# Layernorm statistics: the sum of squares moves from ScalarE to VectorE, and the negated mean times rstd moves the other way

## The chip, the cores and the metric

The kernel runs on the 8 cores of one Trainium2 chip. Each core takes one batch element of the input (4096 tokens of 1024 features) and runs the same program. No core waits for another. The time is the device time of the slowest core in microseconds (us), and smaller is better.

## What is computed

One layer of two sub-layers, each with a layernorm in front and a layernorm behind, and a residual. The layernorm has no gain and no bias:

```python
def _layernorm(x, axis=-1, eps=1e-5):
    m = jnp.mean(x, axis=axis, keepdims=True)
    v = jnp.var(x, axis=axis, keepdims=True)
    return (x - m) / jnp.sqrt(v + eps)
...
x = x + _layernorm(_L0_attn_ref(_layernorm(x), W_q, W_k, W_v, W_o))
x = x + _layernorm(_L0_ffn_ref(_layernorm(x), gate_w, We1, ..., Ws2, bs2))
```

`_L0_attn_ref` is causal linear attention with one head of 64: q and k go through elu + 1, a running sum of the outer products of k and v is read out with q and divided by a running normalizer. `_L0_ffn_ref` is a mixture of 16 experts (2 per token, chosen by a softmax gate) and one shared expert, each a gated MLP in a hyperbolic geometry.

## The kernel before

All work is tiled by 128 tokens, one token per partition, so 32 tiles per core. Every instruction is written out once by hand through a helper, `kb.op(engine, emit, after, inc)`: it appends to the list of one engine ("T" TensorE, "V" VectorE, "S" ScalarE, "G" GpSimd, "Y" SyncE, which issues most DMAs), and an engine runs its list strictly in order. `after` holds what the instruction waits for, also where that lies on its own engine. The profile calls the engines PE, DVE, ACT, POOL and SP.

There are four stages, one after another:

- **Stage A1** (`a1_tile` and `a2_chunk`, interleaved by tile). `a1_tile(i)` loads 128 x 1024 of x (L449), takes its statistics with `ln_stats`, normalizes on ScalarE (L456), transposes on TensorE (L462), and makes q, k and v. `phi` (L409 to L418) is elu + 1: VectorE, an Exp on ScalarE (L412), VectorE. `a2_chunk(i-1)` follows with the attention of the tile before it. There are two x buffers and one of nearly everything else.
- **Stage A3** (L603 to L790). For each tile: the output projection into PSUM (L625, L630), a copy to SBUF `s_at` (L642), `ln_stats` over it, x plus bias on ScalarE (L693), the residual on VectorE (L697, a scalar_tensor_tensor of two fp32 SBUF tensors, into `s_x`), `ln_stats` over that result, its normalization on ScalarE (L711), eight fp32 transposes (L721), two copies out of PSUM (L727, L730), and the gate (L747 and the small VectorE operations up to L788).
- **FFN**, in two halves of 16 tiles. It doesn't call `ln_stats`.
- **Final**, after each FFN half, 16 tiles: load x (L1176), `ln_stats` over the FFN output `s_y`, x plus bias on ScalarE (L1181), the residual on VectorE (L1185), the store (L1188). Load and store are issued from the same SyncE list, and the load of a tile stands behind the store of the tile before.

`ln_stats(src_ap, cb, variant, after_src)` writes a few 128x1 columns `C(cb)` to `C(cb+7)` of one small tile `s_c`, and returns rstd and minus mean times rstd. It is called 32 times in A1, 64 times in A3 (variant "expln": Ln, then Exp with factor -0.5, L391 and L394) and 32 times in the final stage (variant "sqrt": Sqrt and reciprocal, L398 and L401). Its two wide operations are the sum (L375, VectorE) and the sum of squares (L378, ScalarE, whose elementwise output goes to the scratch tile `s_sqs`). The small ones are L381 (mean), L384 (its square), L387 (variance) and L403 (minus mean times rstd), all on VectorE.

Beside A1 and the first half of A3, GpSimd converts the fp32 expert weights to bf16: it loads a chunk, casts it from SBUF to SBUF (L284, 128x3328) and stores it, 72 times. The FFN waits for all of it, and for the end of A3.

Of the kernel before, what the change touches and what calls it, by code (L numbers as in the profile page):

```python
# [10 lines left out]
AF = mybir.ActivationFunctionType  # L11
ALU = mybir.AluOpType
AX = mybir.AxisListType

B, T, D, H = 8, 4096, 1024, 64
# [176 lines left out]
def build_nc(debug=False, stop_after=None, a3_gate=True, a3_xtspill=True,  # L192
# [4 lines left out]
    kb = KB(nc, es)  # L197
# [38 lines left out]
    chV = kb.chan("chV", "V")  # L236
    chS = kb.chan("chS", "S")
# [7 lines left out]
    s_sqs = es.enter_context(st("s_sqs", [128, D], BF16))  # L245
# [17 lines left out]
    def C(i):  # L263
        return s_c[:, i:i + 1]
# [59 lines left out]
    for dsrc, dst in ((d_wq, s_wqb), (d_wk, s_wkb), (d_wv, s_wvb)):  # L324
        tin = kb.op("Y", lambda y, s=dsrc: y.dma_start(out=s_wst[:, 0:512], in_=s),
                    after=(prev[0],), inc=chL[0], k=16)
        tcv = kb.op("G", lambda gp, d=dst: gp.tensor_copy(out=d[:, :], in_=s_wst[:, 0:512]),
                    after=(tin,), inc=chGc)
# [3 lines left out]
                after=(prev[0],), inc=chL[0], k=16)  # L332
    tcv = kb.op("G", lambda gp: gp.tensor_copy(out=s_wob[:, :], in_=s_wst[:64, 0:1024]),
                after=(tin,), inc=chGc)
# [4 lines left out]
    if stop_after == "W":  # L339
        kb.op("G", lambda g: g.nop(),  # L340
              after=(prev[0], prev[1], t_consts[0]))
# [32 lines left out]
    def ln_stats(src_ap, cb, variant, after_src):  # L374
        t1 = kb.op("V", lambda v: v.tensor_reduce(  # L375
            out=C(cb), in_=src_ap, axis=AX.X, op=ALU.add),
            after=after_src, inc=chV)
        t2 = kb.op("S", lambda s: s.activation(  # L378
            out=s_sqs[:, :], in_=src_ap, func=AF.Square, accum_out=C(cb + 1)),
            after=after_src, inc=chS)  # L380
        t3 = kb.op("V", lambda v: v.tensor_scalar(  # L381
            out=C(cb + 2), in0=C(cb), scalar1=1.0 / D, scalar2=None,
            op0=ALU.mult), after=(t1,), inc=chV)
        t4 = kb.op("V", lambda v: v.tensor_tensor(  # L384
            out=C(cb + 3), in0=C(cb + 2), in1=C(cb + 2), op=ALU.mult),
            after=(t3,), inc=chV)
        t5 = kb.op("V", lambda v: v.scalar_tensor_tensor(  # L387
            out=C(cb + 4), in0=C(cb + 1), scalar=1.0 / D, in1=C(cb + 3),
            op0=ALU.mult, op1=ALU.subtract), after=(t2, t4), inc=chV)
        if variant == "expln":  # L390
            t6 = kb.op("S", lambda s: s.activation(  # L391
                out=C(cb + 5), in_=C(cb + 4), func=AF.Ln, bias=c_epsln),
                after=(t5, t_cst), inc=chS)
            t7 = kb.op("S", lambda s: s.activation(  # L394
                out=C(cb + 6), in_=C(cb + 5), func=AF.Exp, scale=c_mhalf),
                after=(t6,), inc=chS)
        else:
            t6 = kb.op("S", lambda s: s.activation(  # L398
                out=C(cb + 5), in_=C(cb + 4), func=AF.Sqrt, bias=c_epsln),
                after=(t5, t_cst), inc=chS)  # L400
            t7 = kb.op("V", lambda v: v.reciprocal(  # L401
                out=C(cb + 6), in_=C(cb + 5)), after=(t6,), inc=chV)
        t8 = kb.op("V", lambda v: v.tensor_scalar(  # L403
            out=C(cb + 7), in0=C(cb + 2), scalar1=C(cb + 6), scalar2=-1.0,
            op0=ALU.mult, op1=ALU.mult), after=(t7, t4), inc=chV)
        return C(cb + 6), C(cb + 7), (t7, t8)

    def phi(src_ap, dst_ap, w, after, np_=128):
# [212 lines left out]
    for i in range(NT):  # L621
        p = i % 2
        cb = 32 * p
# [4 lines left out]
            after=(tok_o[i], g_at[p]) + ((g_of, g_oc) if i < 2 else ()),  # L628
            inc=None)
        t2 = kb.op("T", lambda t, i=i, atp=atp: t.matmul(  # L630
            atp[:, 512:1024], s_of[0:64, i * 128:(i + 1) * 128],
            s_wob[:, 512:1024], start=True, stop=True), after=(), inc=chT)
        if a3_level < 2:
            tev = kb.op("V", lambda v, atp=atp, p=p: v.tensor_copy(
                out=s_w32[:, p * D:(p + 1) * D], in_=atp[:, :]),
                after=(t2, g_at[p], g_w32[p]), inc=chV)
# [6 lines left out]
            out=atsl, in_=atp[:, :]), after=(t2, g_at[p], g_atS[p]), inc=chV)  # L643
        g_at[p] = tat
        if 11 <= a3_level <= 15:
            toks = []
            t1 = kb.op("V", lambda v, atsl=atsl, cb=cb: v.tensor_reduce(
                out=C(cb), in_=atsl, axis=AX.X, op=ALU.add),
                after=(tat,), inc=chV)
            toks.append(t1)  # L650
            if a3_level >= 12:
                t2s = kb.op("S", lambda s, atsl=atsl, cb=cb: s.activation(
                    out=s_sqs[:, :], in_=atsl, func=AF.Square,
                    accum_out=C(cb + 1)), after=(tat,), inc=chS)
                toks.append(t2s)
            if a3_level >= 13:
                t3 = kb.op("V", lambda v, cb=cb: v.tensor_scalar(
                    out=C(cb + 2), in0=C(cb), scalar1=1.0 / D, scalar2=None,
                    op0=ALU.mult), after=(t1,), inc=chV)
                t4 = kb.op("V", lambda v, cb=cb: v.tensor_tensor(  # L660
                    out=C(cb + 3), in0=C(cb + 2), in1=C(cb + 2), op=ALU.mult),
                    after=(t3,), inc=chV)
                t5 = kb.op("V", lambda v, cb=cb: v.scalar_tensor_tensor(
                    out=C(cb + 4), in0=C(cb + 1), scalar=1.0 / D,
                    in1=C(cb + 3), op0=ALU.mult, op1=ALU.subtract),
                    after=(t2s, t4), inc=chV)
                t8 = kb.op("V", lambda v, cb=cb: v.tensor_scalar(
                    out=C(cb + 7), in0=C(cb + 2), scalar1=C(cb + 4),
                    scalar2=-1.0, op0=ALU.mult, op1=ALU.mult),
                    after=(t5,), inc=chV)  # L670
                toks += [t8]
            if a3_level >= 14:
                t6 = kb.op("S", lambda s, cb=cb: s.activation(
                    out=C(cb + 5), in_=C(cb + 4), func=AF.Ln, bias=c_epsln),
                    after=(t5, t_cst), inc=chS)
                t7 = kb.op("S", lambda s, cb=cb: s.activation(
                    out=C(cb + 6), in_=C(cb + 5), func=AF.Exp, scale=c_mhalf),
                    after=(t6,), inc=chS)
                toks += [t7]
            tev = kb.op("V", lambda v, atsl=atsl, p=p: v.tensor_copy(  # L680
                out=s_w32[:, p * D:(p + 1) * D], in_=atsl),
                after=tuple(toks) + (g_w32[p],), inc=chV)
# [7 lines left out]
            out=xsl, in_=d_x[i * 128:(i + 1) * 128, :]),  # L690
            after=(g_x[p],), inc=chX[p], k=16)
        wsl = s_w32[:, p * D:(p + 1) * D]
        txf = kb.op("S", lambda s, xsl=xsl, wsl=wsl, mb=mb: s.activation(  # L693
            out=wsl, in_=xsl, func=AF.Identity, bias=mb),
            after=(tx, tln[1], g_w32[p]), inc=chS)
        tx2 = kb.op("V", lambda v, atsl=atsl, xsl=xsl, wsl=wsl, rstd=rstd:
                    v.scalar_tensor_tensor(  # L697
                        out=xsl, in0=atsl, scalar=rstd, in1=wsl,
                        op0=ALU.mult, op1=ALU.add),
                    after=(txf, tln[0]), inc=chV)  # L700
        g_atS[p] = tx2
        tok_x2sp[i] = kb.op("Y", lambda y, i=i, xsl=xsl: y.dma_start(
            out=d_x2[i * 128:(i + 1) * 128, :], in_=xsl),
            after=(tx2,), inc=chSp[p], k=16)
        if a3_level < 3:
# [6 lines left out]
                                   scale=rstd2, bias=mb2),  # L712
                      after=tln2 + (txf,), inc=chS)
# [6 lines left out]
        for k in range(8):  # L720
# [3 lines left out]
                after=(tln2f, g_tr2) if k == 0 else (),  # L724
                inc=chT if k == 7 else None)
        g_w32[p] = ttr
        tfm32 = kb.op("V", lambda v: v.tensor_copy(  # L727
            out=s_fm32[:, :], in_=p_tr2[:, :]), after=(ttr, g_fm32), inc=chV)
        bsl = s_b16[:, p * D:(p + 1) * D]
        txtb = kb.op("V", lambda v, bsl=bsl: v.tensor_copy(  # L730
            out=bsl, in_=p_tr2[:, :]),
            after=(ttr, g_b16[p], tfm32), inc=chV)
        g_tr2 = txtb
        if a3_xtspill:
            tok_xtsp[i] = kb.op("Y", lambda y, i=i, bsl=bsl: y.dma_start(
                out=d_xt[:, :, i * 128:(i + 1) * 128].rearrange("k p n -> p k n"),
                in_=bsl.rearrange("p (k n) -> p k n", k=8)),
                after=(txtb,), inc=chXt[p], k=16)
# [7 lines left out]
        for k in range(8):  # L746
# [3 lines left out]
                after=(tfm32, g_gate) if k == 0 else (),  # L750
                inc=chT if k == 7 else None)
# [3 lines left out]
            out=gsl, in_=p_gate[:, :]), after=(tg, g_gate), inc=chV)  # L755
        tmx = kb.op("V", lambda v, cb=cb, gsl=gsl: v.reduce_max(
            out=C(cb + 16), in_=gsl, axis=AX.X), after=(tgc,), inc=chV)
        tnm = kb.op("V", lambda v, cb=cb: v.tensor_scalar(
            out=C(cb + 17), in0=C(cb + 16), scalar1=-1.0, scalar2=None,
            op0=ALU.mult), after=(tmx,), inc=chV)  # L760
# [3 lines left out]
            out=esl, in_=gsl, func=AF.Exp, bias=C(cb + 17)),  # L764
            after=(tnm,), inc=chS)
        g_gate = tgc
        tse = kb.op("V", lambda v, cb=cb, esl=esl: v.tensor_reduce(
            out=C(cb + 18), in_=esl, axis=AX.X, op=ALU.add),
            after=(te,), inc=chV)
        trs = kb.op("V", lambda v, cb=cb: v.reciprocal(  # L770
            out=C(cb + 19), in_=C(cb + 18)), after=(tse,), inc=chV)
        tm1 = kb.op("V", lambda v, cb=cb, esl=esl: v.reduce_max(
            out=C(cb + 20), in_=esl, axis=AX.X), after=(te,), inc=chV)
        teq = kb.op("V", lambda v, cb=cb, esl=esl, bsl2=bsl2: v.tensor_scalar(
            out=bsl2, in0=esl, scalar1=C(cb + 20), scalar2=None,
            op0=ALU.is_equal), after=(tm1,), inc=chV)
        tmk = kb.op("V", lambda v, esl=esl, bsl2=bsl2: v.scalar_tensor_tensor(
            out=bsl2, in0=bsl2, scalar=-1e30, in1=esl,
            op0=ALU.mult, op1=ALU.add), after=(teq,), inc=chV)
        tm2 = kb.op("V", lambda v, cb=cb, bsl2=bsl2: v.reduce_max(  # L780
            out=C(cb + 21), in_=bsl2, axis=AX.X), after=(tmk,), inc=chV)
        th = kb.op("V", lambda v, cb=cb, esl=esl, i=i: v.tensor_scalar(
            out=s_hit[:, i * 16:(i + 1) * 16], in0=esl, scalar1=C(cb + 21),
            scalar2=None, op0=ALU.is_ge), after=(tm2,), inc=chV)
        tw1 = kb.op("V", lambda v, cb=cb, esl=esl, bsl2=bsl2: v.tensor_scalar(
            out=bsl2, in0=esl, scalar1=C(cb + 19), scalar2=None,
            op0=ALU.mult), after=(trs, tm2), inc=chV)
        tw2 = kb.op("V", lambda v, i=i, bsl2=bsl2: v.tensor_tensor(  # L788
            out=s_wte[:, i * 16:(i + 1) * 16], in0=bsl2,
            in1=s_hit[:, i * 16:(i + 1) * 16], op=ALU.mult),  # L790
            after=(th, tw1), inc=chV)
# [6 lines left out]
    if stop_after == "A":  # L798
        kb.op("G", lambda g: g.nop(), after=a_done)
        with nc.Block() as block:  # L800
# [21 lines left out]
                   after=a_done, inc=chGc)  # L822
    t_ones_time = kb.op("G", lambda g: g.memset(s_timeb[:, :], 1.0),
                        after=a_done, inc=chGc)
# [285 lines left out]
    for h in range(2):  # L1110
        yg = tuple(t for t in g_y if t is not None)
        ty0 = kb.op("G", lambda g: g.memset(s_y[:, :], 0.0),
                    after=yg + ((a_done) if h == 0 else ()), inc=chGc)
        ty1 = kb.op("G", lambda g: g.memset(
            bass.AP(s_y, 0, [[NLT * D, 128], [D, NLT], [1, 1]]), 1.0),
            after=(ty0,), inc=chGc)
# [52 lines left out]
        for lt in range(NLT):  # L1169
            gi = h * NLT + lt  # L1170
            px = lt % 2
            cb = 32 * px + 16
# [4 lines left out]
                out=xsl, in_=d_x2[gi * 128:(gi + 1) * 128, :]),  # L1177
# [55 lines left out]
```

How the kernel before makes its waits and increments, by code:

```python
            def section(eng, items=items, engname=engname):  # L91
                waited = {}
                for _, after, emitfn, inc, k, idx in items:
                    for (ch, tidx) in after:
                        if ch.owner == engname == "T":
                            continue
                        val = val_at[(ch.name, tidx)]
                        if waited.get(ch.name, 0) < val:
                            eng.wait_ge(ch.sem, val)
                            waited[ch.name] = val
                    instr = emitfn(eng)
                    if inc is not None:
                        if instr is None:
                            instr = eng.nop()
                        instr.then_inc(inc.sem, k)
```

## Time and profile before

| | us |
|---|---|
| device time, median of 2 runs | 7313.36 (7301.6 to 7325.12) |
| device time of the profiled execution | 7106.19 |
| its span, slowest core | 7104.5 |
| spans of the 8 cores | 7075.2 to 7104.5 |
| mean granted TensorE clock of the cores | 0.761 to 0.775 |
| busy: PE, DVE, ACT, POOL | 4617.9, 3785.3, 3425.4, 322.4 |

The profile is of one execution, 207 us shorter than the median of the timed runs. Its busy shares (PE 65%, DVE 53%, ACT 48%) are means over stages that have nothing in common: A1 takes about 22 to 632 us, A3 632 to 1383 us, the two FFN halves about 1400 to 4118 and 4260 to 6982 us, and the two final stages 4118 to 4243 and 6982 to 7104.5 us. So what an edit is worth is read stage by stage. "Waits" of an engine are put down to the instruction whose semaphore came last.

### The profile page before, as it was taken

The numbers are of one execution on the slowest core, as the hardware profiler recorded it, in microseconds if no ns is written. First come the engines' busy times: TensorE is split into PE (matmuls) and PEld (weight loads), VectorE is DVE, ScalarE is ACT, GpSimd is POOL, SyncE is SP. The second block draws the span as 40 slices with busy tenths as digits, with TensorE's granted clock in tenths as the row PEclk, the third lists the DMA queues.
The fourth block names the chain that finished last, engine by engine and source line by source line (L and its number), as shares of the span: only waits on it lengthen the run. The fifth ranks groups of instructions, "written<-read, shape, count | busy, mean of one in ns | idle before, by whom it ended". The sixth has DMA issues, their size and how long they took to land.

```text
span 7104.5 us, 86704 instructions; the slowest of 8 cores (7075.2 to 7104.5 us)
## 1 busy us (share of the span) xinstructions
PE 4617.9 (65%) x27904; PEld 2811.3 (40%) x27904; DVE 3785.3 (53%) x8768; ACT 3425.4 (48%) x6077; POOL 322.4 (5%) x238
## 2 busy tenths in 40 slices
PE   2232222387777887777886718877778887778672
PEld 2222222254444454444553405544445544445350
DVE  3444554455555555555554345555555555555434
ACT  1112222255555555565554335556655555565434
POOL 2222210000000000000000000000000000000000
PEclk8555555588888888887887858888878888888786
DMA  5666741211111111111111031111111111121102
GB/s 208 221 222 222 239 157 59 96 53 50 44 44 66 51 54 47 44 44 66 53 33 52 13 124 64 53 47 44 44 67 55 53 44 44 44 69 33 55 16 92
DMA packets 371414, 547.20 MB, mean 77 GB/s; under 512 B 48338, under 2 KB 327250, under 8 KB 357394
## 3 DMA queue, kind: packets, MB, share of 16 engines
q1 hardware_dynamic: 350226, 358.49, 15.7%
q0 software_dynamic: 20736, 183.18, 7.2%
q8 instruction: 224, 3.67, 0.2%
q14 instruction: 228, 1.87, 0.1%
HBM read 438.62 MB, written 103.00 MB: 76 GB/s over the span
## 4 chain that ended last, share of the span: by engine, by line
ACT 34%; PE 32%; DVE 19%; issue 10%; DMA 3%; DVEq 1%; ACTq 1%; SPq 1%; POOL 0%; POOLq 0%
ACT s_sqs L1029 9%; ACT s_sqs L1054 9%; ACT s_y L1087 8%; PE psA L896 5%; PE psB L896 5%; PE psB L907 5%; PE psA L907 5%; PE p_s1C L896 2%; DMA s_x<-x2sp 2%; DVE s_c L1077 2%; DVE s_c L375 2%; ACT s_c L1068 2%; PE p_s3C L907 2%; PE p_gate L747 2%; ACT s_sq L945 1%
## 5 line engine op out<-in xcount | busy, mean ns | idle before, releaser
L1001 PE MATMUL psB<-s_we,s_sf 128*128 128x512 bf16 (+1 forms) x2048 | 679.0, 490 | 310.5 <-DVE s_w L1042 310.5
L1001 PE MATMUL psA<-s_we,s_sf 128*128 128x512 bf16 (+1 forms) x2048 | 687.6, 496 | 286.3 <-DVE s_w L1042 265.0
L1087 ACT ACTIVATE s_y<-s_w,s_c 128x1024 f32<-128x1024 f32 x544 | 624.6, 1148 | 356.2 <-DVE s_c L1077 353.1
L924 ACT ACTIVATE s_a<-s_s1f,s_beb 128x256 bf16<-128x256 f32 x1152 | 490.8, 496 | 532.9 <-DVE s_s1f L918 531.7
L896 PE MATMUL psA<-s_xtb,s_we 128*128 128x256 bf16 x4096 | 544.3, 299 | 228.7 <-DMA s_xtb<-xtsp 171.9
L945 ACT ACTIVATE s_sq<-s_sf 128x1024 bf16<-128x1024 bf16 (+1 forms) x272 | 301.0, 1107 | 761.6 <-DVE s_sf L940 744.5
L907 PE MATMUL psA<-s_xtb,s_we 128*128 128x256 bf16 x4096 | 536.0, 296 | 168.4 <-DVE s_w L1042 168.4
L1029 ACT ACTIVATE s_sqs<-s_b 128x1023 bf16<-128x1023 bf16 x544 | 575.3, 1058 | 96.3 <-DVE s_b L1026 95.2
L896 PEld LDWEIGHTS psA<-s_xtb,s_we 128*128 128x128 bf16 x4096 | 428.5, 107 | 353.8 <-issue 272.8
L1054 ACT ACTIVATE s_sqs<-s_w 128x1023 bf16<-128x1023 f32 x544 | 566.8, 1042 | 0.5
L907 PEld LDWEIGHTS psA<-s_xtb,s_we 128*128 128x128 bf16 x4096 | 432.9, 106 | 255.5 <-issue 176.0
L1001 PEld LDWEIGHTS psB<-s_we,s_sf 128*128 128x128 bf16 x2048 | 218.3, 116 | 748.7 <-issue 645.9
L1001 PEld LDWEIGHTS psA<-s_we,s_sf 128*128 128x128 bf16 x2048 | 220.5, 117 | 723.7 <-issue 625.8
L896 PE MATMUL psB<-s_xtb,s_we 128*128 128x256 bf16 x4096 | 469.1, 273 | 1.9 <-DMA s_xtb<-xtsp 1.9
L907 PE MATMUL psB<-s_xtb,s_we 128*128 128x256 bf16 x4096 | 468.1, 273 | 0.0
L896 PEld LDWEIGHTS psB<-s_xtb,s_we 128*128 128x128 bf16 x4096 | 393.1, 98 | 67.8 <-issue 23.9
L907 PEld LDWEIGHTS psB<-s_xtb,s_we 128*128 128x128 bf16 x4096 | 401.1, 98 | 46.1
L1026 DVE CAST s_b<-psA 128x1023 bf16<-128x1023 f32 x256 | 312.3, 1220 | 145.0 <-PE psA L1011 143.6
L721 PE MATMUL p_tr<-s_idf,s_w 128*128 128x128 f32 x256 | 62.1, 424 | 495.2 <-ACT s_w L711 495.2
L1068 ACT ACTIVATE s_c<-s_c 128x1 f32<-128x1 f32 x544 | 110.3, 203 | 490.3 <-DVE s_c L1066 490.3
L933 DVE TENSOR_SCALAR s_s3b<-psB,s_beb 128x256 bf16<-128x256 f32 x512 | 212.2, 477 | 229.8 <-PE psB L907 224.4
L933 DVE TENSOR_SCALAR s_s3b<-psA,s_beb 128x256 bf16<-128x256 f32 x512 | 212.2, 477 | 228.8 <-PE psA L907 228.8
(171 smaller groups left out, 6523.7 us busy)
## 6 DMA issues: line engine op xcount, KB each, us to landing
s_xtb<-xtsp SPq DMA_DIRECT2D x272, 512.0 KB, 3.8
s_we<-wec SPq DMA_DIRECT2D x32, 3326.8 KB, 11.5
s_wst<-wexp POOLq DMA_DIRECT2D x48, 1664.0 KB, 8.9
wec<-s_wsb POOLq DMA_DIRECT2D x48, 832.0 KB, 4.5
s_x<-x SPq DMA_DIRECT2D x64, 512.0 KB, 5.0
s_wst<-wexp POOLq DMA_DIRECT2D x16, 1661.5 KB, 9.3
x2sp<-s_x SPq DMA_DIRECT2D x32, 512.0 KB, 2.6
s_x<-x2sp SPq DMA_DIRECT2D x32, 512.0 KB, 4.3
```

Of the source, the lines that this page charges most:

```text
L375: t1 = kb.op("V", lambda v: v.tensor_reduce(out=C(cb), in_=src_ap, axis=AX.X, op=ALU.add), after=after_src, inc=chV)
L896: t.matmul(s1r[:, it * GRP:(it + 1) * GRP], wsl[:, w1o + k * stride1 + it * 128: w1o + k * stride1 + it * 128 + 128], xsl[:, k * GRP:(k + ...
L907: t.matmul(s3r[:, it * GRP:(it + 1) * GRP], wsl[:, w3o + k * stride1 + it * 128: w3o + k * stride1 + it * 128 + 128], xsl[:, k * GRP:(k + ...
L924: s.activation(out=s_a[:, it * GRP:(it + 1) * GRP], in_=s_s1f[:, (it - it0) * GRP:(it - it0 + 1) * GRP], func=AF.Silu, bias=bsl[:, it:it + ...
L933: v.tensor_scalar(out=s_s3b[:, it * GRP:(it + 1) * GRP], in0=s3r[:, it * GRP:(it + 1) * GRP], scalar1=bsl[:, nit + it:nit + it + 1], scala ...
L945: tsq = kb.op("S", lambda s, sfo=sfo, nit=nit, pg=pg: s.activation(out=s_sq[:, pg * 2048:pg * 2048 + nit * GRP], in_=s_sf[:, sfo:sfo + nit ...
L1001: wnh=wnh, pob=pob: t.matmul(pob(nh * 512, nh * 512 + wnh), s_sf[:, sfo + kt * GRP + tt * 128: sfo + kt * GRP + tt * 128 + 128], wsl[:, w2 ...
L1026: v.tensor_copy(out=bscr, in_=pob(0, NSH)),
L1029: s.activation(out=s_sqs[:, 0:NSH], in_=bscr, func=AF.Square, accum_out=C(cb)),
L1054: tS1 = kb.op("S", lambda s, zsl=zsl, cb=cb: s.activation(out=s_sqs[:, 0:NSH], in_=zsl[:, 1:D], func=AF.Square, accum_out=C(cb + 2)), afte ...
L1068: tsq2 = kb.op("S", lambda s, cb=cb: s.activation(out=C(cb + 7), in_=C(cb + 6), func=AF.Sqrt), after=(trc,), inc=chS)
L1087: s.activation(out=ysl, in_=zsl, func=AF.Identity, scale=rcol),
```

## The change

Only `ln_stats` changes. The sum of squares becomes a VectorE scalar_tensor_tensor, (x * 1.0) * x, with an accumulator output. The mean column becomes the negated mean. In the variant "expln" the product of negated mean and rstd is now a ScalarE Identity with a per-partition scale; in the variant "sqrt" it stays on VectorE. The square of the mean and the variance are computed as before.

```diff
-        t2 = kb.op("S", lambda s: s.activation(
-            out=s_sqs[:, :], in_=src_ap, func=AF.Square, accum_out=C(cb + 1)),
-            after=after_src, inc=chS)
+        t2 = kb.op("V", lambda v: v.scalar_tensor_tensor(
+            out=s_sqs[:, :], in0=src_ap, scalar=1.0, in1=src_ap,
+            op0=ALU.mult, op1=ALU.mult, accum_out=C(cb + 1)),
+            after=after_src, inc=chV)
         t3 = kb.op("V", lambda v: v.tensor_scalar(
-            out=C(cb + 2), in0=C(cb), scalar1=1.0 / D, scalar2=None,
+            out=C(cb + 2), in0=C(cb), scalar1=-1.0 / D, scalar2=None,
             op0=ALU.mult), after=(t1,), inc=chV)
...
             t7 = kb.op("S", lambda s: s.activation(
                 out=C(cb + 6), in_=C(cb + 5), func=AF.Exp, scale=c_mhalf),
                 after=(t6,), inc=chS)
+            t8 = kb.op("S", lambda s: s.activation(
+                out=C(cb + 7), in_=C(cb + 2), func=AF.Identity,
+                scale=C(cb + 6)), after=(t7,), inc=chS)
         else:
...
             t7 = kb.op("V", lambda v: v.reciprocal(
                 out=C(cb + 6), in_=C(cb + 5)), after=(t6,), inc=chV)
-        t8 = kb.op("V", lambda v: v.tensor_scalar(
-            out=C(cb + 7), in0=C(cb + 2), scalar1=C(cb + 6), scalar2=-1.0,
-            op0=ALU.mult, op1=ALU.mult), after=(t7, t4), inc=chV)
+            t8 = kb.op("V", lambda v: v.tensor_scalar(
+                out=C(cb + 7), in0=C(cb + 2), scalar1=C(cb + 6), scalar2=None,
+                op0=ALU.mult), after=(t7,), inc=chV)
```

## Rows read from the trace of the kernel before

**Rows 1.** Busy time by stretch: stretch, its length, then each engine's busy us (instructions).

```profile
22.00:632.00 610.00, 187.02 (x1794) 147.00 (x1794) 275.03 (x897) 119.52 (x257) 185.03 (x138) 0.61 0.62 222
...
1000.00:1372.00 372.00, 103.80 (x417) 82.93 (x416) 179.58 (x438) 104.03 (x187) 0.00 (x0) 0.50 0.19 59
```

**Rows 2.** Chain of waits, one tile of A3: start us, us, what.

```profile
1143.44 1.30 DVE s_x L697
...
1144.83 1.23 DVE s_c L375
...
1161.24 1.23 DVE s_c L375
...
1164.13 0.23 DVE s_c L403
...
1165.75 1.29 DVE s_x L697
```

**Rows 3.** Timeline of the same ln_stats in A3: start us, us, engine line operation.

```profile
1161.23 1.06 ACT L378 ACTIVATE s_sqs<-s_at 128x1024 bf16<-128x1024 f32 x1 [3.51 <-DVE s_at L642]
...
1162.19 0.19 ACT L378 ACTIVATION_READ_ACCUMULATOR s_sqs<-s_at 128x1 f32 x1
1162.56 0.15 DVE L381 TENSOR_SCALAR s_c<-s_c 128x1 f32<-128x1 f32 x1
...
1163.34 0.29 ACT L391 ACTIVATE s_c<-s_c,s_cst 128x1 f32<-128x1 f32 x1 [0.96 <-DVE s_c L387]
1163.73 0.29 ACT L394 ACTIVATE s_c<-s_c,s_cst 128x1 f32<-128x1 f32 x1
...
1164.49 1.15 ACT L693 ACTIVATE s_w<-s_x,s_c 128x1024 f32<-128x1024 f32 x1 [0.47 <-DVE s_c L403]
```

**Rows 4.** Timeline of an ln_stats in A1, and the square of the next tile.

```profile
419.33 1.20 DVE L375 TENSOR_REDUCE s_c<-s_x 128x1 f32<-128x1024 f32 x1
420.64 0.15 DVE L381 TENSOR_SCALAR s_c<-s_c 128x1 f32<-128x1 f32 x1
...
432.10 1.04 ACT L378 ACTIVATE s_sqs<-s_x 128x1024 bf16<-128x1024 f32 x1
```

**Rows 5.** Durations by line: ns min/median/max, first and last start us.

```profile
L697 DVE SCALAR_TENSOR_TENSOR s_x<-s_at,s_c,s_w x32: 1283/1285/2472, 637.4 to 1367.0; 128x1024 f32<-128x1024 f32 x32
...
L387 DVE SCALAR_TENSOR_TENSOR s_c<-s_c 128x1 f32<-128x1 f32 x34 | 5.4, 160 | 3.9 <-DVE s_c L384 0.5
...
L378 ACT ACT_TABLE_LOAD  x1: 1283/1283/1283, 22.9 to 22.9; - x1
```

**Rows 6.** Timeline, two wide VectorE operations with no wait between them (FFN).

```profile
4099.00 1.23 DVE L1026 CAST s_b<-p_s1C 128x1023 bf16<-128x1023 f32 x1
4100.14 1.21 DVE L1042 SCALAR_TENSOR_TENSOR s_w<-p_s1C,s_y 128x1023 f32<-128x1023 f32 x1
```

**Rows 7.** A cast of GpSimd beside VectorE in A1 (timeline), and all casts by line.

```profile
398.31 2.96 POOL L284 CAST s_wsb<-s_wst 128x3328 bf16<-128x3328 f32 x1 [7.88 <-DMA s_wst<-wexp]
...
398.79 2.48 DVE L384 TENSOR_TENSOR s_c<-s_c 128x1 f32<-128x1 f32 x1
...
L284 POOL CAST s_wsb<-s_wst x72: 2102/2960/3225, 30.2 to 987.3; 128x3328 bf16<-128x3328 f32 x55, 128x3323 bf16<-128x3323 f32 x16, 128x2295 bf16<-128x2295 f32 x1
```

**Rows 8.** Groups by line, 22:632, then 632:1000: count, busy us, mean ns.

```profile
L384 DVE TENSOR_TENSOR s_c<-s_c 128x1 f32<-128x1 f32 x32 | 27.6, 864 | 3.3
...
L384 DVE TENSOR_TENSOR s_c<-s_c 128x1 f32<-128x1 f32 x30 | 22.9, 762 | 3.3 <-DVE s_c L381 0.3
```

**Rows 9.** Timeline of a tile of the final stage; the last row is another tile.

```profile
4210.72 1.21 DVE L375 TENSOR_REDUCE s_c<-s_y 128x1 f32<-128x1024 f32 x1
...
4213.48 0.21 DVE L403 TENSOR_SCALAR s_c<-s_c 128x1 f32<-128x1 f32 x1
4215.89 1.15 ACT L1181 ACTIVATE s_w<-s_x,s_c 128x1024 f32<-128x1024 f32 x1 [2.78 <-DMA s_x<-x2sp]
...
7088.83 1.15 ACT L1181 ACTIVATE s_w<-s_x,s_c 128x1024 f32<-128x1024 f32 x1 [2.24 <-DMA s_x<-x2sp]
```

## The prediction, made before the changed kernel was run

> **What bounds the kernel now.** The change touches only `ln_stats`, so I first cut the span at the calls of it, with the busy time by stretch [rows 1]. In A1 (22 to 632 us) PE is busy 187 of 610 us, DVE 275 and ACT 120. In the later part of A3 it is alike: 104, 180 and 104 of 372 us. No engine is near its limit, so these stages are bound by a chain in which one engine at a time works. The two long FFN stretches hold no `ln_stats`; I expect nothing there.
>
> Second, the chain of waits for one tile of A3 [rows 2]. From one residual operation L697 to the next it is 1143.44 to 1165.75, 22.31 us, a tile of A3. Both calls of `ln_stats` lie on the chain: the sum L375 at 1144.83 and at 1161.24, and L403 at 1164.13. The square L378 is nowhere on it.
>
> Third, the timeline, to see why the square is off it [rows 3]. In A3 it starts at 1161.23, together with the sum. Its accumulator is read by 1162.38, before the sum ends (1161.24 + 1.23 = 1162.47). In A1 the square of a tile even runs before its sum: at 432.10, while DVE is busy with the tile before [rows 4]. So in both stages the square is work on ACT that costs nothing today.
>
> **The new square on DVE.** It has the same start condition as the sum and stands right behind it, so now it stands in line with it. The price of the instruction: L697 is a scalar_tensor_tensor over two fp32 SBUF inputs of 1024 columns and takes 1285 ns [rows 5]; it reads its scalar from SBUF. The new one has an immediate scalar. L403 has its scalar in SBUF and takes 0.21 us [rows 9] where L381 with an immediate takes 0.15 [rows 3], so some 60 ns come off: 1.225 us, which is also what the wide sum takes. Two wide DVE operations with no wait between them overlap: L1042 starts 1.14 us behind the start of L1026, which lasts 1.23 [rows 6].
>
> Then the start of the next instruction, L381. Today it is 1.32 us behind the start of the sum (1161.24 to 1162.56 [rows 2, 3]; in A1 419.33 to 420.64 [rows 4]), since it waits for the sum's result. After the change the sum takes 1.14 us to the start of the square, and the square 1.14 us to L381, which waits for nothing any more: 2.28. That is 0.96 us more. To it comes the read of the accumulator. No row shows one on DVE. The nearest is ACT's: it starts 0.10 us before the square ends and lasts 0.19 [rows 3], so it adds 0.09. From below it is 0. From above it is a small DVE operation with a full wait in front, 0.16 + 0.10 and a little more, say 0.35. I take 0.09, by the nearest row: **1.05 us per call** (0.96 to 1.31). L384 and L387 follow as before; the squares' sum is there by the time L387 needs it (two small operations later).
>
> On the path: 32 calls in A1 and 64 in A3, 96 x 1.05 = 100.8 us (92 to 126).
>
> **The product on ACT.** Today from the start of L394 to the start of L693 it is 1163.73 to 1164.49, 0.76 us, with a hop to DVE and back [rows 3]. After the change L394 is followed by another small ACT operation and then by the wide one. The step from one small ACT operation to the next that waits for it is 0.39 us (L391 to L394 [rows 3]). Twice that is 0.78, so +0.02 per call, 96 x 0.02 = 2 us: the hop saved and the operation added cancel. The new Identity reads an SBUF operand besides its input, as L391 and L394 do, so I keep their price. It could be a tenth of a microsecond cheaper (as a DVE operation with an immediate is 0.06 cheaper than one without) or 0.02 dearer: -7 to +4.
>
> **The table load.** ACT's first table load now stands before L391 of the first tile instead of beside the first sum [rows 5], 1.28 us, of which some was already on the path: +1, once.
>
> **GpSimd's casts.** A small DVE operation with two SBUF inputs that becomes due during a cast waits for its end: L384 at 398.79 lasts 2.48 us and ends at 401.27, the very end of the cast that began at 398.31 [rows 7]. The new square has two SBUF inputs. There are 72 casts in 957 us [rows 7], 0.075 per us. L384 loses (864 - 160) x 32 = 22.5 us in A1 and (762 - 160) x 30 = 18.1 us in A3 up to 1000 us [rows 8]. Three parts: a cast that hit L384 now hits the square, due some 0.45 us earlier, about 9 casts, +4 us. A cast that comes due during the square waits for it and then holds L384 for up to 2.7 us: 62 squares (32 in A1, 30 in A3 [rows 8]) x 1.23 us x 0.075 = 5.7 casts at 2.5 = +14 us. And the longer tiles take up casts that would have cost about 1 us each elsewhere (62 x 1.05 x 0.075 = 5): -5. Sum **+13 us** (0, if the casts fall between, to 25). GpSimd itself is no path: its last cast starts at 987 us [rows 7], and L697 still runs at 1367 [rows 5].
>
> **The final stage.** The load of x ends the wait there: L1181 starts at 4215.89 on the DMA, and L403 has been ready since 4213.69 [rows 9]. That leaves 2.2 us of cover for 1.05 more. In a tile with a faster load ACT sat idle 2.24 us instead of 2.78, so 1.66 us of cover. Without this cover it would cost 32 x 1.05 = 34 us. I take 0.
>
> **What ACT gains**: 128 squares of 1.04 to 1.06 us and their reads, 128 x (1.05 + 0.19) = 159 us of busy time off ACT. But all of it ran while ACT would have waited anyway [rows 2 to 4]. Worth 0.
>
> **Sum**: 100.8 + 2 + 1 + 13 = 117 us. Against the profiled execution: 7106.2 + 117 = 7223. The timed runs' median is 207 us above it; I can't tell from the trace where those lie, and both A stages are chains of fixed latencies, so I add the same 117 to the median: 7313.4 + 117 = **7430 us**, +1.6%. From the bounds: 92 - 7 + 0 + 0 = 85 to 126 + 4 + 1 + 25 = 156 us, and 12 us either way for the scatter of the two runs around their median: 7386 to 7481.
>
> **Rivals.**
>
> *The accumulating form runs at half the rate.* For: no row shows a DVE operation with an accumulator, and it has to keep two fp32 streams and a running sum. Against: L697 has the same two streams and shows one column per cycle. Its price: the width-dependent part of the square is 1.225 - 0.160 (L387, one column [rows 5]) = 1.065 us, so it comes on top once more: 2.12 us per call, 96 x 2.12 = 203 us. Casts hit a square twice as long: 25 us. The final stage's cover of 1.66 to 2.2 us is used up in part, about 3 us. With 2 and 1 it is 234 us: 7547 us, +3.2%, slower. It decides from 1.35 us per call on ((146 - 16) / 96, where 146 us are 2%).
> The Trainium skill says this in so many words (Vector Engine (DVE) Microarchitecture Reference, section Points that are easy to get wrong): a scalar_tensor_tensor with two non-bf16 SBUF sources runs at half throughput, since both read ports are taken and none is left for the accumulator. The trace does not bear out the first half of it: L697 with two fp32 SBUF sources takes 1285 ns for 1024 columns, not some 2.3 us. Whether an accumulator output brings it about no run here shows; that is what keeps this rival at more than a few per cent.
>
> *The square is hidden.* If it cost nothing, 7313. For: DVE is busy under half of these stages. Against: the sum right before it and L403 behind it are both on the chain [rows 2]. In A1 it could only hide if DVE ran it before the sum while waiting for PE, but it stands behind the sum, which stands behind the last tile's work.
>
> *The tables.* If Ln and Exp landed in different table sets now that no Square comes first, there would be two loads of 1.28 us in each of 96 calls, 246 us more: 7676. Against: today Ln and Exp run 96 times with a single load in all of A1 and A3 [rows 5].
>
> **How the numbers follow.** Forecast (0.96 to 1.31 us per call) 0.80; half rate 0.12; hidden, or something freed on ACT that I don't see, 0.04; tables 0.02; casts much worse than I reckon 0.02. The range of the forecast holds 8 in 10, so it is the range, 7386 to 7481. A measurement of this kernel tells about 2% (146 us) from no change. Slower by more than that: the half rate, the tables, the casts and the upper end of the forecast (0.11), together 0.27. Faster by over 2%: 0.01. Within 2%: 0.72.
>
> **What would show it.** In the profile of the changed kernel: a wide DVE operation at L378's place of about 1.22 us with a short accumulator read; from the start of the sum to the start of the negated mean about 2.4 us where it was 1.32; a tile of A3 without casts 24.4 to 24.5 us long instead of 22.3; the first FFN matmul some 117 us later; ACT busy some 130 us less (159 less 96 small operations of 0.29); the two FFN stretches and the final stages as long as before. I am wrong if the square takes over 1.5 us, if a table load stands between Ln and Exp, or if the FFN stretches change.

## The result, and the profile after

| | before | after |
|---|---|---|
| ratio of the times, 95% interval | | 1.0129 (1.0083 to 1.0175) |
| device time of the profiled execution, us | 7106.19 | 7218.57 |
| span, mean of the 8 cores, us | 7088.4 | 7193.4 |
| median of all timed runs, us | 7167.91 (10 runs) | 7344.12 (11 runs) |
| busy PE, DVE, ACT, us | 4617.9, 3785.3, 3425.4 | 4612.0, 3896.2, 3313.4 |

The change makes the kernel 1.3% slower, some 92 us of 7106. In part of the executions, of either kernel, the cores of one die or of both show a lower granted TensorE clock (0.72 against 0.76 in the one of 7344.12 us) and the time is 1 to 5% longer, so the ratio leaves those executions out, and by their times the two behind the 7313 us that stood ahead of the prediction are among them.

To see where the time goes I use one mark that every core has: the first clearing of `s_y` by GpSimd, which waits for the end of A3. Here is its row in before, by line (count, ns min/median/max, start of the first and of the last, of the slowest core):

```profile
L1112 POOL MEMSET s_y<- x2: 13745/13748/13751, 1385.6 to 4243.9; 128x16384 f32 x2
```

The same row in after, also of the slowest core:

```profile
L1116 POOL MEMSET s_y<- x2: 13745/13748/13751, 1479.0 to 4342.8; 128x16384 f32 x2
```

| mean of the 8 cores, us | before | after | difference |
|---|---|---|---|
| A3 begins (first L642, now L646) | 627.0 | 664.6 | +37.6 |
| A3 ends (first clearing of `s_y`) | 1380.8 | 1473.2 | +92.4 |
| second half begins (second clearing) | 4230.5 | 4329.6 | +99.1 |
| end of the span | 7088.4 | 7193.4 | +105.0 |

So 92 us arise in A1 and A3. The other 13 us lie in the two FFN halves, where the program is the same. In before the rest of the program behind A3 took 5708 us and in after 5720. In the profiled executions of the experiments below that leave this part alone it took 5698 to 5721 us (5698 in prod_act_only, 5707 in sq_dve_only, 5721 in sums_act_dmacast1), and 5769 and 5761 in before_dmacast and before_dmacast1, where after_dmacast, with the same edit, took 5719. That is no relation to the edits, so I put these 13 us down to the scatter between executions. The final stages stayed as they were: from their first to their last wide ScalarE operation 113.3 us before and 112.8 after in the first half, 111.1 and 112.3 in the second (means of the cores).

The timeline of after shows the same stretch of a tile of A3 as [rows 2] and [rows 3] (lines behind L378 are shifted: L381 is now L382, L387 L388, L391 L392, L394 L395, L693 L697, L697 L701; L398 is the new product):

```profile
1234.24 1.22 DVE L375 TENSOR_REDUCE s_c<-s_at 128x1 f32<-128x1024 f32 x1
1235.37 1.22 DVE L378 SCALAR_TENSOR_TENSOR s_sqs<-s_at 128x1024 bf16<-128x1024 f32 x1
1236.51 0.08 DVE L378 DVE_READ_ACCUMULATOR s_sqs<-s_at 128x1 f32 x1
1236.51 0.15 DVE L382 TENSOR_SCALAR s_c<-s_c 128x1 f32<-128x1 f32 x1
...
1237.03 0.16 DVE L388 SCALAR_TENSOR_TENSOR s_c<-s_c 128x1 f32<-128x1 f32 x1
1237.29 0.29 ACT L392 ACTIVATE s_c<-s_c,s_cst 128x1 f32<-128x1 f32 x1 [6.57 <-DVE s_c L388]
1237.67 0.29 ACT L395 ACTIVATE s_c<-s_c,s_cst 128x1 f32<-128x1 f32 x1
1238.06 0.29 ACT L398 ACTIVATE s_c<-s_c 128x1 f32<-128x1 f32 x1
1238.50 1.15 ACT L697 ACTIVATE s_w<-s_x,s_c 128x1024 f32<-128x1024 f32 x1
1239.76 1.29 DVE L701 SCALAR_TENSOR_TENSOR s_x<-s_at,s_c,s_w 128x1024 f32<-128x1024 f32 x1 [2.57 <-ACT s_w L697]
```

From the start of the sum to the start of the mean it is now 2.27 us (1234.24 to 1236.51); it was 1.32 [rows 3]. The square is in line, 0.95 us per call. The read of the accumulator is an instruction of its own of 0.08 us, but it has the same start as L382: it costs nothing. From the Exp to the wide operation it is 0.83 us (1237.67 to 1238.50) where it was 0.76 [rows 3].

By line, the square of after and its accumulator read (ns min/median/max):

```profile
L378 DVE SCALAR_TENSOR_TENSOR s_sqs<-s_x x64: 1202/1215/3683, 25.0 to 1462.0; 128x1024 bf16<-128x1024 f32 x64
L378 DVE DVE_READ_ACCUMULATOR s_sqs<-s_x x64: 70/77/84, 26.1 to 1463.1; 128x1 f32 x64
```

The median is 1215 ns for 1024 columns. The maximum of 3683 is a square that waited for a cast, as the small operation L384 did in [rows 7].

### The profile page after: what moved, and what is told of

The parts are those of the page before. It is cut to its first block, busy times and chain, and to the rows that moved or that the text cites. A ratio compares the mean times of both kernels' runs of the same rounds, so it can differ in the third digit from the quotient of the medians.

```text
span 7217.0 us, 86276 instructions; the slowest of 8 cores (7178.0 to 7217.0 us)
## 1 busy us (share of the span) xinstructions
PE 4612.0 (64%) x27764; PEld 2822.4 (39%) x27904; DVE 3896.2 (54%) x8928; ACT 3313.4 (46%) x5917; POOL 326.9 (5%) x238
## 4 chain that ended last, share of the span: by engine, by line
ACT 34%; PE 32%; DVE 18%; issue 12%; DMA 3%; DVEq 1%; ACTq 1%; SPq 0%; POOL 0%; POOLq 0%
ACT s_sqs L1033 9%; ACT s_sqs L1058 9%; ACT s_y L1091 8%; PE psA L900 5%; PE psB L900 5%; PE psB L911 5%; PE psA L911 5%; PE p_s1C L900 2%; DMA s_x<-x2sp 2%; DVE s_c L375 2%; DVE s_c L1081 2%; PE p_gate L751 2%; ACT s_c L1072 2%; PE p_s3C L911 2%; ACT s_sq L949 1%
## 5 line engine op out<-in xcount | busy, mean ns | idle before, releaser
L1005 PE MATMUL psB<-s_we,s_sf 128*128 128x511 bf16 (+1 forms) x1984 | 675.4, 500 | 331.6 <-DVE s_w L1046 326.5
L1005 PE MATMUL psA<-s_we,s_sf 128*128 128x511 bf16 (+1 forms) x1984 | 663.5, 493 | 292.1 <-DVE s_w L1046 258.4
L1030 DVE CAST s_b<-psA 128x1023 bf16<-128x1023 f32 x256 | 312.3, 1220 | 150.0 <-PE psA L1015 148.6
```

The lines of the kernel that those rows point to most:

```text
L1005: wnh=wnh, pob=pob: t.matmul(pob(nh * 512, nh * 512 + wnh), s_sf[:, sfo + kt * GRP + tt * 128: sfo + kt * GRP + tt * 128 + 128], wsl[:, w2 ...
L1030: v.tensor_copy(out=bscr, in_=pob(0, NSH)),
```

## Experiments

Each kernel below differs from the kernel before, or from the changed one, by the edit shown. The mark is again the end of A3, the mean of the 8 cores of the profiled execution. In the kernels in which GpSimd casts, the 8 cores end A3 up to 25 us apart, so such a mean is known to 2 or 3 us (its standard error); where the DMAs cast one at a time in before_dmacast1 and after_dmacast1 they lie within 4.4 us, and the mean is known to 0.6.

| kernel | A3 begins | A3 ends | span |
|---|---|---|---|
| before | 627.0 | 1380.8 | 7088.4 |
| after | 664.6 | 1473.2 | 7193.4 |
| sq_dve_only | 664.2 | 1470.6 | 7177.6 |
| prod_act_only | 633.6 | 1387.6 | 7085.8 |
| before_dmacast | 575.0 | 1335.9 | 7105.1 |
| after_dmacast | 608.4 | 1403.1 | 7121.8 |
| before_dmacast1 | 575.1 | 1295.0 | 7056.1 |
| after_dmacast1 | 608.8 | 1392.1 | 7107.3 |
| final_3sq | 665.9 | 1474.6 | 7248.8 |
| a1_sum_act | 575.4 | 1335.9 | 7042.6 |
| sums_act | 576.8 | 1233.5 | 6941.2 |
| sums_act_dmacast | 537.4 | 1227.6 | 6948.7 |
| sums_act_dmacast1 | 537.0 | 1161.2 | 6882.5 |

### The two halves of the change, each alone

sq_dve_only takes only the first edit of the diff (the square on VectorE). prod_act_only takes only the negated mean and the product on ScalarE.

> Kernel before with the one edit that the sum of squares is the VectorE scalar_tensor_tensor with an accumulator output; mean and product as before. Measure: start of GpSimd's first clearing of s_y (it waits for the end of A3), mean of the 8 cores: 1380.8 us in the kernel before, 1473.2 in the changed one (+92.3). Theory (the square stands in line on VectorE, 0.95 us per call, 96 calls, and GpSimd's casts add nothing net): +85 to +91, so 1466 to 1472, and the start of the sum to the start of the mean 2.27 us. Rival (the hop to ScalarE for the product makes a good part of the loss): below +75.

> Kernel before with the one edit that the mean is negated and the product with rstd runs on ScalarE in the variant expln; the square stays on ScalarE. Theory: the step from the Exp to the wide ScalarE operation grows by 0.06 to 0.07 us, 96 calls, +6 us at the end of A3 (1387). Rival (the hop is cheaper by some 0.1 us, as the saved semaphore would suggest): -5 to -10 us.

Measured: the square alone moves the end of A3 by +89.8 us, the product alone by +6.8 us, both together by +92.4, each give or take some 3 us. The next section takes the scatter of the casts out of these three numbers. The time of sq_dve_only is 1.0143 (1.0098 to 1.0187) of before. The square is the loss; the product is a small second one. The hop that is saved is replaced by an operation that costs as much and a little more. The rivals of both expectations fall.

### The casts taken away

The question here is what GpSimd's casts add to the change. In before_dmacast and after_dmacast the weights are cast by the DMAs, so nothing reads SBUF on GpSimd beside VectorE:

```diff
-        tin = kb.op("G", lambda gp, s=src_ap, pp=p, w=width:
-                    gp.dma_start(out=s_wst[:, pp * CH:pp * CH + w], in_=s), ...)
-        tcv = kb.op("G", lambda gp, pp=p, w=width: gp.tensor_copy(...), ...)
-        tst = kb.op("G", lambda gp, d=dst_ap, pp=p, w=width:
-                    gp.dma_start(out=d, in_=s_wsb[:, pp * CH:pp * CH + w]), ...)
+        tst = kb.op("G", lambda gp, s=src_ap, d=dst_ap:
+                    gp.dma_start(out=d, in_=s),
+                    after=(tok_prev[p],), inc=chCv[p], k=16)
```

> Kernel before, but GpSimd no longer casts the weights from SBUF to SBUF: the 72 chunks are cast by the DMAs on the way from DRAM to DRAM, issued from GpSimd. Same result. Theory (a cast holds each VectorE operation with two SBUF inputs, and all of that lies on the chain of A1 and A3): the small operations like L384 drop to 0.16 us everywhere, and A3 ends some 90 us earlier, near 1290 us. Rival (the stalls lie in waits that would be there anyway): A3 ends within 10 us of 1381. If the casting DMAs are slow and end after A3, the FFN starts late and the time is longer, whatever the stalls.

> The changed kernel with the same edit to the weights as before_dmacast. Theory A (the new square costs the same with and without casts; casts add nothing net): A3 ends 96 x (0.95 + 0.065) = 97 us behind that of before_dmacast. Theory B, my prediction's (+13 us from casts that hit the square): the difference without casts is 13 us smaller than with them, 92 - 13 = 79 us.

Measured: A3 of before_dmacast begins 52.0 us earlier, but ends only 44.9 us earlier, so in A3 it lost 7 us instead of winning some 35. The waits of ScalarE in it say why (who waited for what, us in total, times, longest; the slowest core):

```profile
ACT s_w L686 <- DMA s_x<-x: 45.9, 1, 45.9
```

One load of x at the start of A3, issued at 591.92 us, held ScalarE up for 46 us (38 to 46 on the eight cores), to about the time when the last casting DMAs ended (they are issued up to 636 us). In after_dmacast that wait was 10 to 14 us. So the difference of the two in A3 (33.9 us) says nothing on the casts. A1 has no such wait, and there the difference is +33.4 us without casts and +37.6 with them. The pair doesn't decide between the theories, and its expectation missed this wait.

So the pair was repeated with one casting DMA in flight instead of two:

```diff
-                    after=(tok_prev[p],), inc=chCv[p], k=16)
+                    after=(tok_prev[p], tok_prev[1 - p]), inc=chCv[p], k=16)
```

> before_dmacast with only one casting DMA in flight at a time instead of two (each waits for the one before). Theory (the long wait of one load of x at the start of A3 comes from two casting DMAs crowding the DMA queues, and the stalls behind GpSimd's casts are 86 us): the wait goes, A3 ends 80 to 86 us before 1380.8, near 1297. Rival (any casting DMA holds a load of x until all have ended): the wait grows, since they last longer, and A3 ends behind 1336.

> after_dmacast with one casting DMA in flight. Theory A (each call costs 0.95 + 0.065 us without casts, and the casts took 9 us less in the changed kernel than in the one before): A3 ends 97 to 98 us behind that of before_dmacast1. Theory B (my prediction's +13 us for casts): 79 us.

Measured: the long wait is gone (3.2 us at most on any of the eight cores), and before_dmacast1 ends A3 at 1295.0, 85.9 us before the kernel before. The small operation that [rows 8] shows at a mean of 864 and 762 ns has no stall left in it:

```profile
L377 DVE TENSOR_TENSOR s_c<-s_c x128: 159/160/161, 27.5 to 7106.5; 128x1 f32<-128x1 f32 x128
```

after_dmacast1 ends A3 97.2 us behind before_dmacast1: theory A's 97 to 98, not theory B's 79.

A count from the traces says the same core by core. The mean of each group of VectorE operations in A1 and in A3 is compared with the mean of the same group where nothing casts on GpSimd; what is above it are stalls. Taken off the end of A3 of each core, they leave:

| mean of the 8 cores, us | stalls in A1 | stalls in A3 | end of A3 | end of A3 less the stalls |
|---|---|---|---|---|
| before | 51.8 | 34.0 | 1380.8 | 1295.0 |
| prod_act_only | 56.2 | 29.5 | 1387.6 | 1301.9 |
| sq_dve_only | 57.6 | 27.0 | 1470.6 | 1386.0 |
| after | 55.7 | 25.1 | 1473.2 | 1392.3 |
| final_3sq (the changed kernel up to here) | 57.2 | 25.9 | 1474.6 | 1391.5 |

The last number of before is that of before_dmacast1 (1295.0), and that of after is within 0.2 us of after_dmacast1 (1392.1). On the cores of before it lies between 1293 and 1298, where the ends themselves lie between 1372 and 1388. So all of the stalls lay on the chain. And the change adds up: the square alone costs 91.0 us, which is 96 x 0.95, the product alone 6.9, both 97.3.

With casts the difference at the end of A3 is 92.4 us, so the casts gave back 5 us where I had added 13. By the count it is the same: 80.9 us of stalls instead of 85.8. The minus sign is not firm: the other two executions with the square on VectorE have 83.1 and 84.6 us. The +13 is ruled out by all three.

How can that be, when the mechanism that I priced is there? This is one tile of A3 of the changed kernel, where a cast becomes due during a square:

```profile
889.45 1.22 DVE L375 TENSOR_REDUCE s_c<-s_x 128x1 f32<-128x1024 f32 x1
890.59 1.22 DVE L378 SCALAR_TENSOR_TENSOR s_sqs<-s_x 128x1024 bf16<-128x1024 f32 x1
890.64 3.98 POOL L284 CAST s_wsb<-s_wst 128x3323 bf16<-128x3323 f32 x1 [9.64 <-DMA s_wst<-wexp]
...
891.98 2.65 DVE L385 TENSOR_TENSOR s_c<-s_c 128x1 f32<-128x1 f32 x1
```

The cast takes 3.98 us instead of 2.96, since it waits for the square, and then it holds L385 for 2.65 us instead of 0.16: 2.5 us, just as I had priced it. But such a hit is no addition. By the same count L384 lost 30.8 us in before (the 40.6 that I had read in [rows 8] are of one core, this is the mean of eight); in after L385 loses 8.9 us and the square 26.8, together 4.9 more where I had reckoned 18 (+4 and +14). The other operations lost 55.0 us in before and 45.2 in after, 9.8 less where I had reckoned 5. Read together, these sums say that a cast that hits the square is for the most part one that would have hit another operation. Part of the rest is that the casts run at their own pace and end near 1000 us in either kernel, so the A3 that begins 38 us later sees about 25 of them instead of 27 ((996 - 665) / 13.3 and (987 - 627) / 13.3). How the casts fall from tile to tile was not taken apart further.

### The cover of the final stage

Here the square runs three times in a row, in the variant "sqrt" alone:

```diff
+        if variant != "expln":
+            for _r in range(2):
+                t2 = kb.op("V", lambda v: v.scalar_tensor_tensor(
+                    out=s_sqs[:, :], in0=src_ap, scalar=1.0, in1=src_ap,
+                    op0=ALU.mult, op1=ALU.mult, accum_out=C(cb + 1)),
+                    after=after_src + (t2,), inc=chV)
```

> The changed kernel, but in the final stage (variant sqrt) the square runs three times in a row on VectorE, each behind the one before. Same result. Theory (one square hides in the wait for the load of x, of which 1.66 to 2.2 us is cover): three squares delay the product by 0.95 + 2 x 1.32 = 3.6 us instead of 0.95, so about 1.4 to 1.9 us of each tile show, 21 to 29 us more per final stage (112 us from its first to its last wide ScalarE operation before and after the change). Rival (the final stage is bound by the DMAs' rate, whatever VectorE does): 112 us again.

Measured: from its first to its last wide ScalarE operation a final stage takes 137.6 us in the first half and 137.4 in the second (means of the cores), against 112.8 and 112.3 in the changed kernel: +24.8 and +25.1 us. Both are in the range. The timeline of a tile shows what ends the wait:

```profile
4245.35 0.29 ACT L408 ACTIVATE s_c<-s_c,s_cst 128x1 f32<-128x1 f32 x1 [7.04 <-DVE s_c L394]
...
4246.32 1.15 ACT L1191 ACTIVATE s_w<-s_x,s_c 128x1024 f32<-128x1024 f32 x1 [0.68 <-DVE s_c L413]
```

In [rows 9] L1181 waited for the DMA. Now the same operation waits for the product on VectorE. One square in this stage is free because of 1.7 to 2.2 us of cover, and three are not. The cover itself can be read on one core (core 0, before and after: the wide operation, and what its engine waited for, us in total and times):

```profile
L1181 ACT ACTIVATE s_w<-s_x,s_c x32: 1147/1147/1149, 4122.2 to 7096.1; 128x1024 f32<-128x1024 f32 x32
  DMA s_x<-x2sp: 82.9, 30
...
L1185 ACT ACTIVATE s_w<-s_x,s_c x32: 1147/1147/1148, 4212.5 to 7183.8; 128x1024 f32<-128x1024 f32 x32
  DMA s_x<-x2sp: 49.9, 30
```

The wait for the load is still there after the change, and 33 us shorter: 1.1 us in each of the 30 tiles.

### The opposite direction

If wide work on VectorE is on the chain and wide work on ScalarE is not, the statistics should go to ScalarE. In a1_sum_act the sum of A1 is an Identity on ScalarE with an accumulator output:

```diff
-        t1 = kb.op("V", lambda v: v.tensor_reduce(
-            out=C(cb), in_=src_ap, axis=AX.X, op=ALU.add), ...)
+        t1 = kb.op("S", lambda s: s.activation(
+            out=s_w32[:, 0:D], in_=src_ap, func=AF.Identity,
+            accum_out=C(cb)), after=after_src, inc=chS)
```

> The opposite direction, from the kernel before: in A1 the sum goes to ScalarE too (an Identity with accumulator output into a scratch tile, ahead of the square), A3 and the final stage as before. Theory (wide ScalarE work in A1 runs ahead of its tile and is free, wide VectorE work is on the chain at its full length): a tile of A1 is 1.2 to 1.3 us shorter, A3 starts 39 to 42 us earlier than 627.0, near 586. Rival (ScalarE's second pass gets in the way of the Exp of phi): A3 starts less than 20 us earlier.

Measured: A3 begins 51.6 us earlier, more than the 39 to 42 expected. The same count of stalls finds 37.6 us in its A1 instead of 51.8, so some 14 us of the gain are stalls behind casts, and 37 us, 1.2 per tile, are the sum itself. Without casts it is 38.1 us (575.1 in before_dmacast1, 537.0 in sums_act_dmacast1, whose A1 has the same edit). ScalarE does both passes in the time in which it would have waited:

```profile
307.75 1.04 ACT L376 ACTIVATE s_w<-s_x 128x1024 f32<-128x1024 f32 x1
...
308.79 1.04 ACT L385 ACTIVATE s_sqs<-s_x 128x1024 bf16<-128x1024 f32 x1
...
314.67 0.14 DVE L388 TENSOR_SCALAR s_c<-s_c 128x1 f32<-128x1 f32 x1
```

sums_act adds the same thought for A3. The copy out of PSUM moves to ScalarE and gives its sum, and the residual operation gives the sum of its result:

```diff
-        tat = kb.op("V", lambda v, atp=atp, atsl=atsl: v.tensor_copy(
-            out=atsl, in_=atp[:, :]), after=(t2, g_at[p], g_atS[p]), inc=chV)
+        tat = kb.op("S", lambda s, atp=atp, atsl=atsl, cb=cb: s.activation(
+            out=atsl, in_=atp[:, :], func=AF.Identity, accum_out=C(cb)),
+            after=(t2, g_at[p], g_atS[p]), inc=chS)
...
                         out=xsl, in0=atsl, scalar=rstd, in1=wsl,
-                        op0=ALU.mult, op1=ALU.add),
+                        op0=ALU.mult, op1=ALU.add, accum_out=C(cb + 8)),
```

> From the kernel before: A1 as in a1_sum_act; in A3 the copy of the projection out of PSUM moves to ScalarE with an accumulator output that gives its sum, the residual operation on VectorE gives the sum of its own result through its accumulator output, and both separate sums go. Same result. Theory (what counts is the length of the chain): 40 us in A1; in A3 about 2.2 us per tile for the first call (the copy no longer stands behind the gate's small operations) and 0.5 for the second, 86 us; A3 ends near 1255 us, the time is 1.7% shorter. Rival (ScalarE becomes the chain: copy and square one after the other cost what the sum saved): A3 ends above 1320.

Measured: A3 ends at 1233.5, 147 us earlier, 21 more than expected. Without casts the same edits make it 133.8 us (1295.0 in before_dmacast1, 1161.2 in sums_act_dmacast1), so some 14 us of the 21 came with the casts; the other 8 were not looked into. The device time of the profiled execution is 6950.68 against 7109.88 in one of the kernel before on the same chip, 2.2% less; for this pair there is no interval. The timeline of a tile of A3:

```profile
1156.00 1.00 ACT L649 ACTIVATE s_at<-p_at 128x1024 f32<-128x1024 f32 x1
...
1157.18 1.06 ACT L385 ACTIVATE s_sqs<-s_at 128x1024 bf16<-128x1024 f32 x1
...
1158.17 0.18 DVE L796 TENSOR_TENSOR s_wte<-s_g16b,s_hit 128x16 f32<-128x16 f32 x1
1158.28 0.15 DVE L388 TENSOR_SCALAR s_c<-s_c 128x1 f32<-128x1 f32 x1
```

The copy and the square on ScalarE lie beside the gate's small operations on VectorE, which end at 1158.35. The mean follows at once. In the kernel before a copy and a sum, 2.65 us, stood in between, from the start of this copy to that of L381 at 1162.56 [rows 3]:

```profile
1159.91 1.23 DVE L642 COPY s_at<-p_at 128x1024 f32<-128x1024 f32 x1
```

The last two put the casting DMAs under it:

> sums_act together with the weights cast by the DMAs. Theory: in A1 the 51 us of stalls behind casts go as well, and A3 starts near 535 us; in A3 the stalls (35 us) are traded for a wait of some 45 us for one load of x while the casting DMAs last, as in before_dmacast. A3 ends near 1210 to 1220 us, the time is 2.2% shorter than before.

> sums_act with one casting DMA in flight. Theory: the wait for x goes, A3 ends 60 to 75 us before that of sums_act (1233.5), near 1165, and the time is 3% below the kernel before. Rival (the wait stays as in sums_act_dmacast): A3 ends above 1220.

Measured: with two DMAs in flight A3 begins at 537.4 as expected but ends at 1227.6, behind the 1210 to 1220 expected and only 6 us before sums_act. Not one load of x was late but two in a row, 38 to 58 us the one waited for longest and 71 to 78 us all together, where the expectation had 45. With one in flight A3 ends at 1161.2, 72.3 us before sums_act, as expected. Its time is 0.9663 (0.9552 to 0.9775) of the kernel before, some 3.4% less. It is the fastest version of this study.

## Why the prediction was right or wrong, point by point

**The predicted time, 7430 us with a range from 7386 to 7481: wrong.** The measured median is 7344, but the sum of 117 us isn't what put it outside: with the 92 us measured in place of 117 it would be 7406, inside the range. The step that failed is "I add the same 117 to the median", with "12 us either way for the scatter of the two runs around their median". It took 7313 as what the kernel takes, and 12 us as its scatter, although the profile showed an execution of 7106 us and I had no reading of the 207 us between. The runs showed in its place that ten timed runs of before reach from 7100 to 7379 us with a median of 7168, and eleven of after from 7202 to 7495: which executions fall into a median moves it by far more than 12 us. The sentence "I can't tell from the trace where those lie" should have widened the range down to 7106 + 85 = 7191. The profile alone as the base (7191 to 7262) would have missed the median as well.

Against the profiled execution the text forecast 7223 us, and the profiled execution of the changed kernel took 7218.6. That this is so close is in part luck: 92 of the 112 us between the two executions come from the change, and the rest is scatter behind A3 that happened to fill up what I had too much.

**What bounds A1 and A3: right.** A chain of one engine at a time, with both sums on it and the square beside it. sq_dve_only shows it: 89.8 us (91.0 with the stalls behind casts taken off) for 96 squares that ScalarE had done for nothing.

**The square, 1.05 us per call (0.96 to 1.31): right in kind, 0.10 too large.** The instruction costs 1215 ns (1225 predicted), the step from sum to mean grew by 0.95. The term that was mis-sized is the accumulator's read, taken as 0.09 us after ScalarE's. VectorE's read is 0.08 us long and wholly covered. 96 x 0.95 = 91 us instead of 101, just below the lower end I gave.

**The product on ACT, +2 us: right in kind, too small.** It measured +6.8 us alone, and 6.9 with the stalls taken off (-7 to +4 was the range). I took both steps between dependent ScalarE operations as 0.39 us. From the product to a wide operation that reads it as a bias it is 0.44 (1238.06 to 1238.50).

**The table load, +1 us: borne out within what can be told.** It stands before the first L392 in after, at 26.93 us, for 1.28 us. In A1 without casts the difference is 33.7 us; 32 calls at 0.95 + 0.07 make 32.6.

**The casts, +13 us (0 to 25): wrong.** They measured -5 us (97.2 without casts, 92.4 with them), give or take 3; -1 to -5 by the count in the three executions with the square on VectorE. The step that failed is the +14 for casts that come due during a square: it added such a hit to an average that stays. The event itself is real, 2.5 us each time, but it mostly takes the place of a hit on another operation: +4.9 us on the square and the operation behind it where I had 18, -9.8 on all others where I had -5.

**What ACT gains, 159 us less 28: too large, without effect.** It measured 112 us (3425.4 to 3313.4). I had counted each accumulator read in full, though 0.10 of its 0.19 us lies within the square.

**The final stage, 0: right**, with the cover shown by final_3sq.

**The sum:** 91 + 7 + 1 - 5 = 94, and 92.4 was measured at the end of A3, against 117 forecast. Of the 23 us between 117 and 94, 10 lie in the square, nearly all in the accumulator's read, and 18 in the casts; the product makes up for some 5. The ratio is +1.3%, within 2%, as forecast at 0.72, and on the slow side.

**The rival of half the rate: refuted**, 1215 ns with an accumulator. The Trainium skill (Vector Engine (DVE) Microarchitecture Reference, section Points that are easy to get wrong) states half throughput for a scalar_tensor_tensor with two non-bf16 SBUF sources, with no port left for the accumulator; the measurement differs, with an accumulator output and without (1285 ns, [rows 5]), and it decides. **The rival of hiding: refuted** by sq_dve_only. **The tables:** Ln and Exp follow each other with no load in between, 0.39 us apart (1237.29 and 1237.67), as before.

The casts have a rule in the Trainium skill (SBUF — State Buffer, section Who interferes with whom): a VectorE instruction with two SBUF inputs contends with a GpSimd instruction that reads SBUF, and whichever issues second waits for the whole of the first. The trace agrees both ways, with 2.65 us for L385 behind a cast and 3.98 us for a cast behind a square; and 85.9 us is what it cost this kernel.

## What to carry to other kernels

An engine that is busy for half of a stage is not free in it: in a chain of one engine at a time, what counts is whether an operation lies beside the one that the chain waits for. Balancing busy shares moved 128 squares from where they were free to where 96 of them cost their full length, and the opposite move gained 2.2% (one execution of each). Add a predicted difference to the execution whose profile it was worked out from; where the timed runs stand 3% away from it, find out what those runs are first, or let the range reach to both.

## What the runs showed of the hardware that was not expected

- An accumulator output on a VectorE scalar_tensor_tensor costs no time: its read takes 70 to 85 ns and overlaps the end of the operation and the start of the next. ScalarE's read takes 185 to 189 ns, of which 0.09 us lie behind the end of the square [rows 3].
- With two casting DMAs from DRAM to DRAM in flight, one load of 512 KB of x at the start of A3 held its reader up for 38 to 46 us in before_dmacast, and two in a row for 71 to 78 us together in sums_act_dmacast. With one in flight no load was waited for longer than 5 us, and the 72 casting DMAs took little longer in all: their time to landing fell from 16.6 to 9.4 us in the median, and the last was issued at 671 to 680 us instead of 631 to 636 (cores 0 and 2 of before_dmacast1 and before_dmacast). What holds the loads was not looked into.
- A stall of two engines on SBUF shows in the profile as a long instruction and not as a wait: L384 at 0.16 us in the median and 2.95 at most. A mean well above the median of the same operation is what to look for.
